# Latent attention: the weighted values taken two key blocks at a time, with the projections and rough scores around them reordered

## The reference

```python
c_q  = rmsnorm(x @ Wq_down) * q_norm_w            # 48 wide
c_kv = rmsnorm(x @ Wkv_down) * kv_norm_w          # 64 wide
q, k, v = c_q @ Wq_up, c_kv @ Wk_up, c_kv @ Wv_up # 16 heads x 128
q_rope, k_rope = rope(x @ Wq_rope), rope(x @ Wk_rope)   # 16 heads x 64
scores = (q . k + q_rope . k_rope) * (128 + 64) ** -0.5
out = (softmax(scores) @ v) @ Wout
x = x + out
```

## Time and profile before

| | us |
|---|---|
| median of 3 runs (lowest, highest) | 2196.66 (2193.28, 2201.62) |
| the profiled execution | 2202.58 |
| its span, first to last instruction | 2200.8 |
| PE busy in it | 1992.3 |
| DVE, POOL, ACT busy in it | 1277.8, 866.3, 817.6 |

### The profile page before, as it was taken

How to read it: one execution, slowest core, us unless ns; L and a number is a source line. 1 busy time by engine, 2 the same in 40 slices (tenths; PEclk the granted TensorE clock), 3 DMA queues, 4 the chain that set the end, 5 groups by cost and what they waited for, 6 DMA issues and landing times. The chain is left out here.

```text
span 2200.8 us, 29601 instructions
## 1 busy us (share of the span) xinstructions
PE 1992.3 (91%) x8700; PEld 1251.4 (57%) x8700; DVE 1277.8 (58%) x3064; ACT 817.6 (37%) x1549; POOL 866.3 (39%) x684
## 2 busy tenths in 40 slices
PE   5899869898888789977689999999999999999987
PEld 5676635554554766656545555555565555555556
DVE  6322275777775822227556666666656666667526
ACT  2122244555555212223224444444514444444423
POOL 0344301231212044432025555665425555565632
PEclk9999968999899689998669999999999999999999
DMA  9111232232220811224232212222122222211101
GB/s 389 48 63 63 56 124 29 30 48 39 29 30 1 339 62 60 67 72 155 47 72 58 54 42 51 57 57 57 23 64 58 53 58 57 55 44 47 31 1 51
DMA packets 60587, 150.91 MB, mean 69 GB/s; under 512 B 12976, under 2 KB 18304, under 8 KB 58176
## 3 DMA queue, kind: packets, MB, share of 16 engines
q1 hardware_dynamic: 50208, 120.43, 20.9%
q0 software_dynamic: 9120, 24.92, 3.6%
q10 hardware_dynamic: 1152, 4.19, 0.5%
HBM read 68.95 MB, written 18.61 MB: 40 GB/s over the span
## 5 line engine op out<-in xcount | busy, mean ns | idle before, releaser
L1843 POOL TENSOR_TENSOR mla_PS<-mla_PS,mla_PT 128x1024 f32<-128x1024 f32 x192 | 458.1, 2386 | 199.5 <-ACT mla_PT L2129 198.1
L2272 DVE TENSOR_REDUCE mla_MXP<-PS 128x1 f32<-128x512 f32 x512 | 334.6, 687 | 200.5 <-PE PS L1924 198.3
L2129 ACT ACTIVATE mla_PT<-PS 128x512 f32<-128x512 f32 x512 | 293.5, 599 | 420.6 <-PE PS L1944 372.5
L1953 PE MATMUL PS<-mla_PT,mla_CN 128*64 128x512 f32 x1024 | 274.2, 614 | 0.0
L522 DVE COPY moe_HT<-PS 128x256 f32<-128x256 f32 x188 | 70.7, 418 | 301.5 <-PE PS L648 301.5
L1924 PE MATMUL PS<-mla_KH,mla_QH 113*128 113x512 f32 x512 | 199.4, 456 | 18.1 <-DMA mla_KL<-mla_SL 17.9
L1944 PE MATMUL PS<-mla_QH,mla_KH 113*128 113x512 f32 x512 | 210.2, 411 | 1.7 <-ACT mla_QH L2113 1.5
L1944 PE MATMUL PS<-mla_QH,mla_KL 113*128 113x512 f32 x512 | 201.8, 394 | 0.0
L1944 PE MATMUL PS<-mla_QL,mla_KH 113*128 113x512 f32 x512 | 201.7, 394 | 0.0
L684 POOL DMA_INDIRECT moe_XS<-rows_in,moe_GI x96 | 93.5, 974 | 268.3 <-PE PS L634 132.0
L1149 ACT ACTIVATE att_PT<-PS 128x1024 f32<-128x1024 f32 (+1 forms) x192 | 152.1, 812 | 94.3 <-PE PS L984 92.7
(11 more groups left out here) (295 smaller groups left out, 3188.8 us busy)
## 6 DMA issues: line engine op xcount, KB each, us to landing
W<-in_W_dram SPq DMA_DIRECT2D x16, 2048.0 KB, 27.9
mla_QH<-mla_SH SPq DMA_DIRECT2D x64, 128.0 KB, 2.4
mla_KH<-mla_SH SPq DMA_DIRECT2D x64, 128.0 KB, 2.4
mla_QL<-mla_SL SPq DMA_DIRECT2D x64, 128.0 KB, 2.5
mla_KL<-mla_SL SPq DMA_DIRECT2D x64, 128.0 KB, 2.4
mla_KH<-mla_SH SPq DMA_DIRECT2D x64, 96.0 KB, 2.3
mla_KL<-mla_SL SPq DMA_DIRECT2D x64, 96.0 KB, 2.4
sums_Y<-rows_out SPq DMA_DIRECT2D x9, 512.0 KB, 6.2
```

Source lines behind the costliest of these rows:

```text
L1843: pool.tensor_tensor(PS[:, :], PT[:, slot(0), :] if k == 1 else PS[:, :], PT[:, slot(k), :], ALU.add).then_inc(s_ps.handle, 1)
L1953: ins = pe.matmul(bank(6)[h * DKVL:(h + 1) * DKVL, :], CN[:, b, k, 0:DKVL], PT[:, slot(k), h * HB:(h + 1) * HB], start=(k == 0), stop=(k = ...
L2129: act.activation(PT[:, slot(k), h * HB:(h + 1) * HB], bank(st_bank(s, h))[:, :], ACT.Exp, scale=MLA_SCALE).then_inc(s_p.handle, 1)
L2272: dve.tensor_reduce(MXP[:, n // NPC, c, h, t:t + 1], bank(piece_bank(n))[:, :], AX_X, ALU.max).then_inc(s_mx.handle, 1)
```

## The change

PE takes the values of steps s - 1 and s together in each odd step. The denominators of the half before move in step 0 from behind the first projection to the front of it, and in steps 0 and 8 no values stand beside them any more. There are 24 late pieces (steps 10 to 15, two behind each head's scores) and 8 early ones (steps 2 to 5: 1, 2, 3, 2). Half 0 is projected in steps 0, 1, 1 and half 1 in steps 4, 5, 5; latent keys go to bank E, which they share with early pieces. ACT and DVE take high and low parts in the order latent, even, odd. `products` of half 1 is moved from step 5 to step 4 for one of its two calls. SP places latent rows ahead of rotary rows in each part, high and low.

```diff
-    LATE, EARLY = {9: 2, 10: 4, 11: 4, 12: 4, 13: 4, 14: 4, 15: 4}, {2: 1, 3: 1, 4: 2, 5: 2}
+    LATE, EARLY = {10: 4, 11: 4, 12: 4, 13: 4, 14: 4, 15: 4}, {2: 1, 3: 2, 4: 3, 5: 2}
...
-    piece_bank = lambda n: (A, E)[n % 2] if n >= NLATE else (C, E, B)[n % 3]
+    piece_bank = lambda n: (E, A)[n % 2] if n >= NLATE else (C, E, B)[n % 3]
...
-    half_bank = ((B, C, B), (C, B, C))
+    half_bank = ((C, B, E), (B, C, E))
+    made_as = lambda what: (what + 1) % 3 + 1
...
-                            sp.wait_ge(s_src.handle, s_src.at(6 * it + 3 * half + 2))
+                            sp.wait_ge(s_src.handle, s_src.at(6 * it + 3 * half + made_as(2)))
+                            for h in range(2):
+                                sp.dma_start(f32(k[LAT, buf, h, tok]), src[h * 64:h * 64 + DQL, 2, :]).then_inc(s_kl.handle, 16)
+                            sp.wait_ge(s_src.handle, s_src.at(6 * it + 3 * half + made_as(1)))
                             for h in range(2):
                                 for m, dst in enumerate((q, k)):
                                     i = 32 * (2 * m + h)
                                     sp.dma_start(f32(dst[ROT, buf, h, tok]), src[i:i + 32, 0:2, :]).then_inc(s_kr.handle, 16)
-                        for src, k, s_src in ((SH, KH, s_hi), (SL, KL, s_lo)):
-                            sp.wait_ge(s_src.handle, s_src.at(6 * it + 3 * half + 3))
-                            for h in range(2):
-                                sp.dma_start(f32(k[LAT, buf, h, tok]), src[h * 64:h * 64 + DQL, 2, :]).then_inc(s_kl.handle, 16)
...
+                            if s % 2:
                                 if s == 7:
-                                    project(it + 1, 1, 2)
-                                if s == 14:
+                                    max_rows(it, 1)
+                                if s == NS - 1 and not last:
                                     pe.wait_ge(s_la.handle, s_la.at(2 * it + 1))
                                     max_rows(it + 1, 0)
-                            if s or not first:
-                                values_of(NS * it + s - 1, 2 * it + (s - 1) // TB, (s - 1) % TB)
...
+                                for done in (s - 1, s):
+                                    values_of(NS * it + done, 2 * it + done // TB, done % TB)
...
-                            maxima(near, todo[:1])
-                            if s == 5 and not last:
-                                products(it + 1, 1, 0)
...
+                            maxima(near, todo[:2])
+                            if s == 2 and not last:
+                                lows(it + 1, 0, (0, 1))
+                            if s == 4 and not last:
+                                products(it + 1, 1, 1)
+                            if s == 5:
+                                block_max(it, 1)
+                                if not last:
+                                    products(it + 1, 1, 0)
+                                    rotated(it + 1, 1)
```

## The result

| | us |
|---|---|
| before, median of 4 runs (lowest, highest) | 2199.14 (2193.28, 2203.70) |
| changed, median of 4 runs (lowest, highest) | 2241.03 (2238.14, 2245.40) |
| ratio, 95% interval | 1.0184 (1.0166 to 1.0202) |
| profiled execution, before and changed | 2202.58 and 2238.14 |
| spans of these | 2200.8 and 2236.4 |

The changed kernel is 42 us slower by the medians and 35.6 us by the profiled executions. The forecast was 2213 us, with a range that ended at 2238.

The account below looks back on a forecast made before the run. PE was taken to set the pace, its stalls and saved slots reaching the end one for one. Savings of 39 us against additions of 56 gave net +17: median 2196.7 to 2213 us, range 2190 to 2238.

Parts of the forecast that it names:

- the clock: Rival: granted clock falls in the new stall before piece 31, half clock costing 1.7 us each, +24, 2237 us; chance 12%.
- Values in twos: PE's value groups: each group joined to another saves 0.345 us, 90 groups counted, 31 us saved.
- First late piece: PE's wait for the first late piece goes, as half 1 is projected by step 5: 6 us saved.
- the start: Start of latent attention: latent keys' own bank and two pieces fewer ahead of pair 0 save about 2 us.
- (a) piece 31: PE waits for piece 31 behind DVE's products, which wait for SP's last rotary transfer: 2.8 us in 14 pairs, 39 us.
- (b) denominators: Denominators in step 8 wait for POOL's last sums: 0.5 us in 16 pairs, 8 us.
- (c): Step 3: second values wait for their own exponentials, ACT being busy with high parts: 0.2 us, 14 times, 3 us.
- (d): Late pieces in bursts: the eighth waits for the fifth's maximum on DVE; 0.4 us a pair, 14 times, 6 us.
- t: Start of the last score matmul in step 2; ACT's end of step 3's exponentials was put at t + 3.4.
- 8 groups: Second half of each sequence's last pair: value groups left out of the saving, PE waiting there for POOL's last sum.
- What would show it: Signs named for the profile after, such as PE idle 2 to 3 us before step 5's second rough piece in 14 pairs.
- 2237: Time in us of the rival in which the clock falls, to be shown by clock dips at each pair; chance 12%.

Follow-up runs that it names:

- experiment 10: Changed kernel with products behind the maxima and ACT's high parts behind step 6's exponentials, plus the two steps' values taken apart again: 2255.67 us, 1.0242 of before.
- Experiment 4: Kernel before, with only the values of two steps taken together in the odd steps: 2215.49 us, 1.0074 of before.
- Experiment 3: Changed kernel with eight unused matmuls between pieces 30 and 31, filling the stall: 2222.11 us, 1.0103 of before.
- experiment 1: Changed kernel with SP placing the latent low rows behind the rotary low rows: 2197.78 us, 0.9994 of before.

## Why the prediction was right and wrong

The direction was right, and the place: the stall in front of piece 31 decides, with the chain SP, DVE, PE in the order predicted. The time was 28 us too low. The step that failed is the clock, which the sum put at nothing.

- **Values in twos, -31**: right. 1.86 us for eight records in the trace; experiment 10 prices a group at 0.36 where the prediction took 0.345. The Trainium skill ("TensorEngine Tiling (Array Packing)", Key Properties) says that a change of tiling mode drains the engine, and both numbers have that sign. Experiment 4 adds that joining alone, in the old order, brings waits that cost more than it saves.
- **First late piece, -6, and the start, -2**: the first was right, its wait is gone from every pair but the one at the change of sequence. Of the second, 1.3 us is seen, about the two pieces fewer. The first rough pieces begin at 1107.57 us instead of 1111.41, but 3.7 of that was gained in the stages ahead, in which nothing differs, and the waits that the projections lost are in the 14.9 us for the transfers: the bank of the latent keys brought nothing.
- **(a) piece 31, +39**: right, 2.75 us a pair against 2.8. The landing took 2.49 us where 2.37 was used.
- **(b) denominators, +8**: right, 0.46 us against 0.5.
- **(c) and (d), +9**: wrong, both are 0. With t as in the prediction (1745.33), ACT ends the exponentials of step 3 at t + 3.0 (1748.31), not t + 3.4. In the bursts every piece comes 0.23 us behind the matmul before it, so no maximum is late. Each term was a difference of some tenths between two sums of many terms. They offset a part of the next error.
- **The clock, left out of the sum**: this step failed. The prediction knew the price, 1.7 us a pair, and gave the case 12%, since the clock had stayed up after 2.22 us. One idle stretch that left the clock alone was taken as the likely case for a longer one. After the stalls of 2.5 to 2.6 us it fell in twelve of thirteen pairs, and a dip cost 1.5. Experiment 3 shows it apart from the stall, 19 us in all, and experiment 1 shows it gone with the stall at 1.30 us. With the clock in and (c) and (d) out, the forecast would have been 2213 + 21 - 9 = 2225.
- **What is left**: 16 us by the medians, 7 by the profiled executions (2238 against 2219 + 12), and nearly 11 if the 3.7 us gained in the stages ahead, which the change can't have made, is set aside. 2.5 of the 16 are in the start of the sum: with its fourth run the kernel before has a median of 2199.1, not 2196.7. The third pair, with its stall of 4.16 us and a clock that is still at 0.50 between 1276 and 1278 us, takes 65.6 us instead of 61.5. The change of sequence takes 5.7 us more, where the sum had almost nothing. There PE waits 4.9 us more in all, for DVE 2.59 and 3.09 us instead of 0.99 and 2.22 ahead of two groups of projections, and for ACT 2.7 us instead of 0.9; the clock falls behind both of the waits for DVE, where it did not before. The waits for the last sums of POOL, 1.5 and 2.8 us instead of 0.45 and 1.3, are what the prediction had left out 8 groups for. The change also moves the first projections of the second sequence within the last pair, from steps 9, 11, 12, 13 and 15 to 9, 12 and 13, which neither the description nor the prediction takes up.

The stretch at the change of sequence is 4.1 us longer than before in experiment 4, where only the values are joined, and 5.0 to 7.8 longer in all the others. So none of the edits gives this loss back, and which of the waits makes it was not tested: this part stays open.

Of "what would show it": the idleness in 14 pairs, the products behind the transfer, the denominators' wait, two groups together at the price of the earlier trace rows and no wait for the late piece are all as written. A pair is 61.5 us where about 60 was named. The dips of the clock were named as the sign for 2237, and they are there.

## What to carry to other kernels

A stall in a row of dense matmuls has two prices, its length and the clock behind it; where one stall recurs in each turn of a loop, price both, and let the forecast carry the clock if the trace shows dips after shorter gaps anywhere. Price a wait from start to start, not by the idleness that the list gives it. When an operation is moved in one engine's order, follow it through all engines' orders: the products moved on DVE came back as a wait of PE through ACT, and the cure was a single line there. The saving of joined groups was real, 1.7 us a pair, but only once the two waits that the change brought were removed (2181.6 us, 0.9912 of before). With the denominators moved as well the kernel takes 2174.9 us, 0.9884 (0.9865 to 0.9904).

## What the runs showed of the hardware

TensorE's granted clock fell to 1.2 GHz behind single idle stretches of 2.49 to 2.60 us between dense matmuls in twelve of thirteen pairs of the changed kernel. It fell about when the matmuls restarted or up to 1.5 us later (1694.37), and behind the stall at 1757.54 the slow matmuls ended some 3 us later. Length alone does not decide it: after 2.58 us at 1335.16, and after 2.65 us in experiment 1, it stayed at 2.4 GHz, as it did after 2.15, 1.30 and 0.73 us. After 4.16 us (1271.15) it was at 1.2 GHz until 1278 us at least. At the lower level a matmul of 512 columns had a pitch of 0.43 instead of 0.23 us.

A group of four matmuls with 64-column weights that stands alone among 128-column ones costs 0.35 us to 0.36 us (experiment 10) more than one that is joined to another such group.

A short wait in a row of matmuls costs more than its listed idleness: 0.6 us from start to start for a listed 0.33 (experiment 4).
